# Six of sixteen token-row tables made on GpSimd instead of VectorE

## The reference, cut to what matters

```
t = t + ffn(layernorm(t))
# ffn: router_logits = x @ gate_w.T       (2048 x 8)
#      top 2 of 8 experts by softmax, weights renormalised
#      h = silu(x @ w1[e]) * (x @ w3[e]) ; y = h @ w2[e]
#      out[n] = sum over the two chosen e of weight[n, e] * y[e, n]
```

## Time and profile before

| | |
|---|---|
| median of three timed runs | 772.69 us (770.95 to 772.71) |
| profiled execution | 771.92 us |
| its span, first to last instruction | 770.2 us |
| TensorE matmuls busy | 722.8 us, 94% of the span |
| VectorE busy | 357.9 us, 46% |
| ScalarE busy | 319.6 us, 41% |
| GpSimd busy | 194.6 us, 25% |
| mean granted TensorE clock | 0.966 |

### The profile page before, as it was taken

How to read it: one execution, slowest core, us unless ns; L and a number is a source line. 1 busy time by engine, 2 the same in 40 slices (tenths; PEclk the granted TensorE clock), 3 DMA queues, 4 the chain that set the end, 5 groups by cost and what they waited for, 6 DMA issues and landing times.

```text
span 770.2 us, 9557 instructions
## 1 busy us (share of the span) xinstructions
PE 722.8 (94%) x3544; PEld 586.6 (76%) x3545; DVE 357.9 (46%) x751; ACT 319.6 (41%) x502; POOL 194.6 (25%) x208
## 2 busy tenths in 40 slices
PE   3999999845999999999999999999999999999993
PEld 2777888744778778877888887788888888888883
DVE  6898757785335316332433452244335335432410
ACT  5886565442144334333523442243435334443310
POOL 5336211003601140124022502600351224021011
PEclk9999999855999999999999999999999999999997
DMA  7346777652342733172327415630643275052013
GB/s 249 63 82 110 170 158 153 143 226 72 116 171 102 217 110 113 35 233 75 112 43 245 121 61 135 194 112 15 208 121 113 54 236 149 31 151 28 3 16 40
DMA packets 55970, 92.20 MB, mean 120 GB/s; under 512 B 7536, under 2 KB 40688, under 8 KB 49776
## 3 DMA queue, kind: packets, MB, share of 16 engines
q1 hardware_dynamic: 45728, 71.64, 30.4%
q0 software_dynamic: 9472, 19.43, 12.9%
q10 hardware_dynamic: 720, 0.46, 0.2%
HBM read 65.49 MB, written 17.63 MB: 108 GB/s over the span
## 4 chain that ended last, share of the span: by engine, by line
PE 86%; DVE 7%; DMA 2%; issue 2%; ACT 1%; POOL 1%; SPq 0%; POOLq 0%; DVEq 0%; ACTq 0%
PE bank L927 22%; PE bank L929 22%; PE bank L928 22%; PE bank L830 3%; PE bank L832 3%; PE bank L831 3%; PE bank L997 2%; PE bank L922 2%; PE bank L852 2%; DVE bn L1115 1%; PE bank L1019 1%; PE bank L870 1%; DVE mv L1124 1%; DVE xs_parts L1157 1%; PE bank L845 1%
## 5 line engine op out<-in xcount | busy, mean ns | idle before, releaser
L927 PE MATMUL bank<-xT_hi,w_hi 128*128 128x512 f32 x495 | 193.7, 391 | 1.5 <-DVE xT_lo L1343 1.5
L928 PE MATMUL bank<-xT_lo,w_hi 128*128 128x512 f32 x495 | 193.3, 390 | 0.0
L929 PE MATMUL bank<-xT_hi,w_lo 128*128 128x512 f32 x495 | 193.2, 390 | 0.0
L496 POOL DMA_INDIRECT out_x<-y,dst_i x40 | 63.5, 1587 | 263.1 <-ACT y L697 126.7
L1350 DVE TENSOR_TENSOR h<-bank,h 128x512 f32<-128x512 f32 x64 | 44.3, 692 | 175.1 <-PE bank L929 175.1
L321 DVE TENSOR_TENSOR w_lo<-w_raw,w_hi 128x2048 fp32r<-128x2048 f32 x48 | 109.7, 2287 | 17.6 <-ACT w_hi L316 17.5
L927 PEld LDWEIGHTS bank<-xT_hi,w_hi 128*128 128x128 f32 x495 | 93.3, 188 | 21.2 <-DVE xT_lo L1343 1.8
L929 PEld LDWEIGHTS bank<-xT_hi,w_lo 128*128 128x128 f32 x495 | 93.3, 189 | 19.6
L928 PEld LDWEIGHTS bank<-xT_lo,w_hi 128*128 128x128 f32 x495 | 93.3, 189 | 19.5
L927 PE MATMUL bank<-w_hi,hT_hi 128*128 128x512 f32 x249 | 99.1, 398 | 0.0
L929 PE MATMUL bank<-w_hi,hT_lo 128*128 128x512 f32 x249 | 97.3, 391 | 0.0
(11 more groups left out here) (167 smaller groups left out, 887.4 us busy)
## 6 DMA issues: line engine op xcount, KB each, us to landing
w_raw<-in_units SPq DMA_DIRECT2D x48, 1024.0 KB, 5.3
joint<-xs_parts SPq DMA_DIRECT2D x64, 128.0 KB, 3.8
out_x<-XT SPq DMA_DIRECT2D x17, 256.0 KB, 3.5
XT<-in_x SPq DMA_DIRECT2D x16, 256.0 KB, 6.3
xn_rows<-xnb SPq DMA_DIRECT2D x16, 256.0 KB, 2.5
gate_row<-gate_rows,gate_i POOLq DMA_INDIRECT x40, 2.8
out_x<-y,dst_i POOLq DMA_INDIRECT x40, 5.0
xg<-xn_rows,src_i POOLq DMA_INDIRECT x32, 3.7
```

Source lines behind the costliest of these rows:

```text
L496: pool.indirect_dma_start(out=out, out_offset=bass.IndirectOffsetOnAxis(ap=index, axis=0), in_=rows, in_offset=None, compute_op=ALU.add).t ...
L927: pe.matmul(bank, stationary[0], moving[0], start=start, stop=False)
L928: pe.matmul(bank, stationary[0], moving[1], start=False, stop=False)
L929: return pe.matmul(bank, stationary[1], moving[0], start=False, stop=stop)
```

## The change

A constant `POOL_ROWS = 6` and two semaphores are new. VectorE signals `ranked` when the second batch's ranks are done, before it makes the column table. GpSimd, once the normalised rows are stored, waits for that and makes the row tables 0 to 5 of the second batch; VectorE makes the tables 6 to 15. TensorE waits for both before the second batch's 16 matmuls. The first batch is as before.

```diff
+POOL_ROWS = 6
...
+        ranked, rows_made = sem("ranked"), sem("rows_made")
...
             for n in range(XB):
                 pool.wait_ge(xn_st[n], 16 * NT // XB)
+            pool.wait_ge(ranked, 1)
+            for a in range(POOL_ROWS):
+                t = BATCHES[1][0] + a // 2
+                ins = pool.tensor_scalar(row_token[1][:, a, :], iota[:], rank_f[1][:, 1, a:a + 1], tokid[:, t:t + 1],
+                                         ALU.is_equal, ALU.mult)
+            ins.then_inc(rows_made, 1)
             pool.wait_ge(src_ready, 1)
...
                 pe.wait_ge(slots_hot, g + 1)
+                if g:
+                    pe.wait_ge(rows_made, 1)
...
-                for a in range(NT):
+                for a in range(POOL_ROWS if g else 0, NT):
                     t = BATCHES[g][0] + a // 2
...
             free_sums(range(8, NBLK))
+            dve.sem_inc(ranked, 1)
             hot_columns(1, 0, NT)
```

## The result

The changed kernel takes 774.24 us (773.19 to 774.99, 8 runs) against 771.97 for the kernel before in the same runs: ratio 1.0031, 95% interval 1.0022 to 1.0041. It is slower by about 2.3 us; 771.9 and a small gain were forecast. The profiled execution took 773.19, span 771.5.

What follows compares the result with a forecast made beforehand. TensorE was taken to bound the kernel except in the routing stage, where VectorE's row tables stand in the chain. Tables ending 0.83 us earlier, less TensorE's 0.05, gave a 0.78 gain: 771.9 us, range 770.3 to 774.8.

Steps and rivals of the forecast that it cites:

- What bounds the kernel: TensorE bounds it except in the routing stage, where VectorE's row tables keep it waiting; a microsecond saved there shortens the span.
- The price of a GpSimd table: In the second batch's table stage, one GpSimd row table was taken as 0.40 us, with 0.61 as upper bound.
- three signs against the forecast: In the new profile: GpSimd rows inside the column table, GpSimd steps over 0.49, or a GpSimd row spanning the first weight subtraction.
- VectorE beside GpSimd: GpSimd's six tables start only after VectorE's column table, at 167.31, and then run beside VectorE's ten row tables.
- turn-taking pair of 0.36: In the table stage, one table on each engine takes 0.36 us together, costing VectorE 0.62 us over six pairs.
- whole-row exclusion: Rival in the table stage: VectorE and GpSimd rows exclude each other, pair 0.74, time 774.2; any dearer pair had chance 0.27.
- rival 3: GpSimd starves beside VectorE's tables and first weight subtraction; matmuls start 2.95 us later, 775.7; whole or in part, chance 0.10.
- What is late next: After the tables, first gather and VectorE's second weight subtraction hang on the same index conversion; nothing won or lost there.
- The clock: In the dense products, a clock rise fixed in time would keep half of the 0.78 gain, 772.3; no rival of its own.

## Why the prediction was wrong

- **What bounds the kernel.** Right: the tables were in the chain, and every microsecond of the stage moved the dense start.
- **The price of a GpSimd table is the step that failed.** "I take the two-input row, 0.40" and 0.61 as the upper bound: it is 0.78 alone. The nearest rows were a select and a product; neither has the comparison, and with a sum in its place the table's form is 0.35 shorter. So GpSimd's end was put at 169.5, and its six tables ended 9.65 us after the ranks, 3.03 later than VectorE's sixteen had. Two of the three signs against the forecast came: steps over 0.49, and a GpSimd row across the first weight subtraction.
- **VectorE beside GpSimd.** The column table held GpSimd up to its end, as said. The turn-taking pair of 0.36 did not come: VectorE's ten rows lost 0.14 in place of 0.62. The pair had been read beside GpSimd products with two tensor inputs, and the VectorE row beside the first of them took 1.36 in place of 0.34; a GpSimd table has one tensor input. Whether that is the difference was not tested. The whole-row exclusion kept as a rival was still further off: in 0.86 of a GpSimd table three VectorE tables of 0.26 went by.
- **Hence rival 3, in the part form written there**: a GpSimd step of 0.6 or more, most of it not excluding VectorE. Its point of decision was right, a table left when VectorE's tenth ends, and so was what it loses there: 2.07, nearly the whole subtraction of 2.29. It was given 0.10. With a table at 0.78 to 0.88 from 166.5 on, three are done when VectorE's tenth ends at 169.2; six could not be.
- **What is late next.** "Both hang on the same conversion and move together; nothing is won or lost there" failed: 1.53 us came back, since the added instructions changed which wait the gather itself carries. Without it the changed kernel takes 775.03.
- **The clock** was kept as a matter of half the gain. In both profiles of the changed kernel it rose later after the dense start than in either of the kernel before (5.3 and 5.4 against 3.4 and 4.1), which adds 0.6 to 0.9. The stage is 1.6 to 1.85 longer, the median 2.3 (1.7 to 3.2). Whether the later rise belongs to the change or to the few draws stays open: two versions of the changed kernel, also with six tables, have 4.2 and 3.9, and the kernel before with its waits in the other order has 5.5; with three tables and with the other order of waits the medians also fell by less than the stage did.

The prediction's range held the time and its sign was wrong. That the range held it is luck: its upper end came from whole-row exclusion, which did not happen, and the starving that did happen was left out of it. Without the 1.5 us that the gathers gave back by accident the time is 775.03, outside the range.

## What to carry to other kernels

Before work moves to an engine that has not run the operation, price the operation's own form there: rows of the same shape with another operation were off by a factor of two. Count how many pieces the slower engine ends before the faster one reaches its next long instruction, and give it no more than that: three here, not six. Where an indirect DMA is on the critical path, look at which wait stands on the instruction itself, and at what the other engine starts right behind the event.

## What the runs showed that I had not expected

- A GpSimd gather started 0.29 to 0.31 after the indices when the wait was its own, 0.91 to 0.93 after them when an instruction ahead of it waited.
- On GpSimd a product with a constant (0.53) took longer than a sum and a product with two per-partition scalars (0.43).
- VectorE's row tables, two scalars each, ran beside a GpSimd table almost unhindered (0.34 to 0.43 each), while VectorE's long two-input instructions (128 x 2048, 2.29) stopped one altogether (3.07 and 2.86).
